# Attention in a fused layer: eight of eleven row-sum steps per head group leave TensorE for accumulating transfers into a side buffer

## The reference

```
scores = jnp.einsum('bshd,bthd->bhst', q / jnp.sqrt(jnp.float32(HEAD_DIM)), k)
scores = jnp.where(causal, NEG_INF, scores)
attn = jax.nn.softmax(scores, axis=-1)
ctx = jnp.einsum('bhst,bthd->bshd', attn, v)
```

## Time and profile before

| | |
|---|---|
| median of 3 runs | 2349.49 us (2347.68 to 2350.36) |
| the profiled execution | 2347.9 us, span 2346.0 us |
| busy TensorE / VectorE / ScalarE / GpSimd | 98% / 75% / 55% / 10% of the span |
| attention stage | about 340 to 1525 us |

### The profile page before, as it was taken

The page is one execution under the profiler, slowest core; times in us unless marked ns, Lnnn a source line. Parts: engine busy times, 40 slices in busy tenths (PEclk is TensorE's granted clock), DMA queues, the critical chain, the costliest instruction groups (busy, mean ns, idle before and its releaser), DMA issues.

```text
span 2346.0 us, 34451 instructions
## 1 busy us (share of the span) xinstructions
PE 2305.6 (98%) x12598; PEld 1417.8 (60%) x12598; DVE 1769.3 (75%) x1808; ACT 1295.7 (55%) x1638; POOL 240.5 (10%) x275
## 2 busy tenths in 40 slices
PE   9999989999999999999999999999999999999997
PEld 7888844444444444444444444478888888888886
DVE  7777759899898998989989999945556556465553
ACT  4444458888888888888888888811111111111111
POOL 2111111101111010211102111000000000000001
PEclk9999979999999999999999999999999999999999
DMA  7767794101811008210082101441102011110100
GB/s 248 262 243 254 240 270 97 38 6 28 172 42 41 16 15 168 55 33 24 6 165 67 33 24 40 145 156 37 42 31 66 19 60 36 37 54 19 37 19 20
DMA packets 126303, 197.49 MB, mean 84 GB/s; under 512 B 14489, under 2 KB 39577, under 8 KB 126113
## 3 DMA queue, kind: packets, MB, share of 16 engines
q1 hardware_dynamic: 126128, 195.25, 29.5%
HBM read 122.83 MB, written 72.37 MB: 83 GB/s over the span
## 4 chain that ended last, share of the span: by engine, by line
PE 92%; DMA 2%; ACT 2%; SPq 2%; DVE 2%; issue 1%; POOL 0%; ACTq 0%; DVEq 0%; POOLq 0%
PE score L977 24%; PE ctx_acc L993 21%; PE slot L1384 20%; PE y L1395 10%; PE acc L416 10%; PE slot L1325 3%; PE sums_acc L1001 2%; ACT probs L1052 1%; PE sums_acc L790 1%; PE turn L438 1%; DMA queries<-shift 1%; PE slot L1366 1%; SPq L76 0%; DMA wq_float<-wq_f 0%; DMA v_rows<-v_out 0%
## 5 line engine op out<-in xcount | busy, mean ns | idle before, releaser
L1052 ACT ACTIVATE probs<-score 128x1024 f32<-128x1024 f32 (+3 forms) x1152 | 1000.2, 968 | 174.7 <-PE score L977 171.7
L1113 DVE TENSOR_TENSOR total<-total,probs 128x2048 f32<-128x2048 f32 (+3 forms) x468 | 985.8, 2106 | 76.4 <-POOL probs L941 21.1
L977 PE MATMUL score<-queries,keys 98*128 98x512 f32 (+3 forms) x2304 | 641.8, 406 | 8.6 <-ACT probs L1052 4.3
L977 PEld LDWEIGHTS score<-queries,keys 98*128 98x128 f32 x2304 | 381.0, 189 | 430.5 <-ACT probs L1052 352.0
L1460 ACT ACTIVATE hidden<-slot,gate_scale_sb 128x512 f32<-128x512 f32 x128 | 88.3, 690 | 634.3 <-PE slot L1384 634.3
L993 PE MATMUL ctx_acc<-probs,values 128*32 128x512 f32 (+3 forms) x3584 | 422.3, 561 | 0.0
L1522 DVE SCALAR_TENSOR_TENSOR hidden<-slot,up_scale_sb,hidden 128x512 f32<-128x512 f32 x128 | 96.1, 751 | 255.6 <-ACT hidden L1460 255.6
L941 POOL TENSOR_SCALAR_AFFINE_SELECT probs<-probs 128x512 f32<-128x512 f32 x128 | 158.5, 1240 | 1010.3 <-ACT probs L1052 1010.3
L1384 PE MATMUL slot<-xt_hi,w_front 128*128 128x512 f32 x608 | 238.4, 392 | 1.5 <-DVE xt_lo L1563 1.5
L1384 PE MATMUL slot<-xt_lo,w_front 128*128 128x512 f32 x608 | 238.0, 391 | 0.0
L993 PEld LDWEIGHTS ctx_acc<-probs,values 128*32 128x32 f32 x3584 | 85.4, 108 | 194.1 <-issue 148.0
(11 more groups left out here) (142 smaller groups left out, 2193.8 us busy)
## 6 DMA issues: line engine op xcount, KB each, us to landing
keys<-k_hi SPq DMA_DIRECT2D x64, 256.0 KB
queries<-q_hi SPq DMA_DIRECT2D x64, 256.0 KB
wq_int<-in_wq SPq DMA_DIRECT2D x48, 256.0 KB, 3.3
wq_float<-wq_f SPq DMA_DIRECT2D x48, 256.0 KB, 2.8
x_raw<-in_x_t SPq DMA_DIRECT2D x32, 256.0 KB, 4.2
v_rows<-v_out SPq DMA_DIRECT2D x32, 256.0 KB, 2.1
k_hi<-part_hi SPq DMA_DIRECT2D x32, 256.0 KB, 2.0
k_lo<-part_lo SPq DMA_DIRECT2D x32, 256.0 KB, 2.4
```

Source lines behind the costliest of these rows:

```text
L977: ins = pe.matmul(score[u % RING][:, i, cut(t):], keys[0:ROWS, kb // ST, h, kb % ST * P:(kb % ST + 1) * P], queries[0:ROWS, q_buffer[ch], ...
L1052: act.activation(probs[:, t % PB, 2 * p:2 * p + 2, cut(t):], score[u % RING][:, :, cut(t):], ACT.Exp).then_inc(exped, 1)
L1113: dve.tensor_tensor(into, into, now, ALU.add).then_inc(added, 1)
```

## The change

TensorE keeps three summing steps in each group (`PE_SUMS = 3`), one in chunk 3 and two in chunk 4. In chunks 5 to 7 it has none. There every fourth late step, from the second late step on and none of the last six, is `queued`: places 9, 13, 17 of chunk 5, 9 to 21 of chunk 6, 9 to 25 of chunk 7, so 3 + 4 + 5 = 12 in a group. GpSimd issues a transfer of the step's 128x2048 exponentials, 1 MB, into a new buffer `side`: a plain copy for the first of a chunk, an accumulating transfer for the others, which adds to what is there. Each waits for the one before (`side_added`). ScalarE waits for the transfer before it writes the step's buffer again. Behind the third step from the chunk's end (`fold_at`, place 29 in chunk 7) VectorE adds `side` to `total` once (`folded`), and its next addition waits for that. The memory that is reserved for the descriptors of GpSimd's transfers is set to 4096 bytes, a size that the kernel before does not give.

```diff
-    PE_SUMS = 11
+    PE_SUMS = 3
+    QUEUED_FROM, EVERY, REST = 5, 4, 7
...
-    pe_sums = {late[(i + 1) * len(late) // PE_SUMS - 1] for i in range(PE_SUMS)}
+    early_late = [t for t in late if steps[t][0] < QUEUED_FROM]
+    pe_sums = {early_late[(i + 1) * len(early_late) // PE_SUMS - 1] for i in range(PE_SUMS)}
+    queued = [t for ch in range(QUEUED_FROM, NCH) for t in [x for x in late if steps[x][0] == ch][1:1 - REST:EVERY]]
+    fold_at = {last[ch] - 2: ch for ch in range(QUEUED_FROM, NCH)}
+    NQ, NF = len(queued), len(fold_at)
...
-    adds = [t for t in range(NS) if not by_pe(t)]
+    adds = [t for t in range(NS) if not by_pe(t) and t not in queued]
...
+        side = sb("side", [P, HG, CH])
...
+            def add_aside(g, t):
+
+                ch = steps[t][0]
+                opens = not any(steps[x][0] == ch for x in queued if x < t)
+                if opens:
+                    pool.wait_ge(folded, NF * g + folds_before(ch))
+                else:
+                    pool.wait_ge(side_added, 16 * (NQ * g + queued_before(t)))
+                pool.wait_ge(exped, 2 * NS * g + 2 * t + 2 + RING)
+                pool.nop(nofuse=True)
+                if opens:
+                    pool.dma_start(side[:], probs[:, t % PB, :, :]).then_inc(side_added, 16)
+                else:
+                    pool.dma_start(side[:], probs[:, t % PB, :, :], accum_op=ALU.add).then_inc(side_added, 16)
...
                     act.wait_ge(added, NA * g + adds_before(t - PB + 1) + A_CREDIT)
+                    if t - PB in queued:
+                        act.wait_ge(side_added, 16 * (NQ * g + queued_before(t - PB + 1)))
...
+                            if t - 1 in fold_at:
+                                dve.wait_ge(folded, NF * g + folds_before(ch) + 1)
...
+                    if t in fold_at:
+                        dve.wait_ge(side_added, 16 * (NQ * g + queued_before(last[ch])))
+                        dve.wait_ge(added, NA * g + adds_before(t + 1) + A_CREDIT)
+                        dve.tensor_tensor(total[:, ch % 2, :, :], total[:, ch % 2, :, :], side[:], ALU.add).then_inc(folded, 1)
...
-    nc = bacc.Bacc("TRN2", target_bir_lowering=False, num_devices=1)
+    nc = bacc.Bacc("TRN2", target_bir_lowering=False, num_devices=1, dynamic_dma_scratch_size=4096)
```

More of the change, by code:

```diff
@@ L702, in attend, with queued_before, folds_before @@
     late = [t for t in range(NS) if not diagonal(t) and place(t) >= 2 * ST]
-    pe_sums = {late[(i + 1) * len(late) // PE_SUMS - 1] for i in range(PE_SUMS)}
+    early_late = [t for t in late if steps[t][0] < QUEUED_FROM]
[3 more added lines that the diff above has]
+    NQ, NF = len(queued), len(fold_at)
+    assert not any(t in queued or t in pe_sums for t in fold_at)
+    def queued_before(t):
+        return sum(x < t for x in queued)
+    def folds_before(ch):
+        return max(0, ch - QUEUED_FROM)
     def by_pe(t):
         return t in pe_sums
-    adds = [t for t in range(NS) if not by_pe(t)]
+    adds = [t for t in range(NS) if not by_pe(t) and t not in queued]
     NA = len(adds)
@@ L751, in attend @@
         begun = sem("begun")
+        side_added = sem("side_added")
+        folded = sem("folded")
         totaled = sem("totaled")
@@ L933, in pool_attention, with mask @@
                             .then_inc(g_masked, 1)
+            def mask(g, t):
+                pool.wait_ge(exped, 2 * NS * g + 2 * t + 2 + RING)
+                view = probs[:, t % PB, :, cut(t):cut(t) + P]
+                pool.nop(nofuse=True)
+                pool.affine_select(out=view, in_=view, compare_op=ALU.is_ge, fill=0.0, base=0,
+                                   pattern=[[0, HG], [1, P]], channel_multiplier=-1).then_inc(masked, 1)
+            def add_aside(g, t):
[5 more added lines that the diff above has]
+                    pool.wait_ge(side_added, 16 * (NQ * g + queued_before(t)))
+                pool.wait_ge(exped, 2 * NS * g + 2 * t + 2 + RING)
+                pool.nop(nofuse=True)
+                if opens:
+                    pool.dma_start(side[:], probs[:, t % PB, :, :]).then_inc(side_added, 16)
+                else:
+                    pool.dma_start(side[:], probs[:, t % PB, :, :], accum_op=ALU.add).then_inc(side_added, 16)
             for g in range(NG):
@@ L936, in pool_attention @@
                     if diagonal(t):
[L938 to L942, removed]
+                        mask(g, t)
+                    elif t in queued:
+                        add_aside(g, t)
         def pe_attention(pe, general):
@@ L1104, in dve_attention @@
                     ch, kb = steps[t]
-                    if not by_pe(t) and (place(t) or not ch):
+                    if t in adds and (place(t) or not ch):
                         dve.wait_ge(exped, 2 * NS * g + 2 * t + 2 + RING)
```

## The result

| | before | changed |
|---|---|---|
| median | 2349.34 us (4 runs) | 2403.19 us (4 runs, 2402.58 to 2406.29) |
| ratio | | 1.0233, 95% interval 1.0221 to 1.0245 |
| profiled execution, span | 2347.9, 2346.0 us | 2403.6, 2401.8 us |

The change makes the kernel 54 us slower. Forecast were 25 us less, and the range ended at 2400.

A forecast was written before the change was run, and what follows sets the result against it. TensorE was taken to set the pace, VectorE a close second. 2347.9 - 27.5 (removed sums) + 2 (VectorE) = 2322.4 us profiled, so 2324 us median; own range 2317 to 2334, whole range 2317 to 2400 us.

The forecast's parts named there:

- The removed sums: Chunks 5 to 7: 32 summing steps fewer at 0.86 us, 27.5 us saved (1.72, 1.72, 3.44 us per chunk).
- The small bound: Lower figure for the removed sums from the matmul rows: 0.52 us a step, 16.7 us for 32 steps.
- VectorE: Chunks 5, 6, 7: VectorE needs 47.9, 54.2, 64.0 us against TensorE's 48.6, 56.75, 64.4, so it fits.
- The charge of 2 us: 0.5 us added for each group for a chunk start where VectorE's work doesn't fit; bounds nothing to 12 us.
- the two rivals on them: GpSimd issues lengthen additions by 0.48 us each: 2335 us, chance 0.07; issues wait up to 2.29 us for additions: 2362 us, 0.05.
- D where nothing competes: Time from a queued step's exponentials' end to its transfer's landing, chunks 5 and 6: 7.7 us, within the 8.25 us spacing.
- the prediction's other estimate: Accumulating transfer by the skill's fixed time and rate, at half rate: 2.0 + 2 x 2.4 = 6.8 us.
- I charge nothing: Chunk 7: accumulating transfers get a good part of the engines on their own queue, loads become late instead; 0 us.
- The first rival: Chunk 7, groups 0 to 2: loads hold transfers up, D 13.4 us, 40 us lost, 2364 us; chance 0.22.

The follow-up runs named there:

- chunk 4: Version for chunks 5 and 6 (TensorE sums four steps in chunk 7, nothing queued there) with two queued steps in chunk 4 too: 2328.98 us, ratio 0.9917.
- the kernel for chunks 5 and 6: The changed kernel with queued steps in chunks 5 and 6 alone; in chunk 7 TensorE sums four steps as before: 2338.17 us, ratio 0.9950.

## Why the prediction was wrong

- **The removed sums: right.** 0.86 us each, from the two lengths of a cycle. Chunk 5 lost 1.51, chunk 6 1.68 us, as 1.72 said; chunk 7 is at 64.47 us when the loads are small, 64.4 predicted. The small bound was misread: the 352 records of the matmul row are eight for each of 44 steps, so it gives 1.04 us a step and 33 us for 32, not 0.52 and 16.7, and is no lower bound. By the same count the 48 matmuls that the prediction expected in the trace are 96 records.
- **VectorE: right that it fits,** with the reason too narrow. I compared its occupancy with each chunk's length; it carries additions over, as chunk 4 showed. The charge of 2 us wasn't needed for chunks 5 to 7, though chunks 3 and 4, where a TensorE sum moved, grew by 0.2 to 0.5 us each, 2.05 us in all: that the charge of 2 us comes out is luck.
- **The issues and VectorE: the two rivals on them have fallen.** In the changed kernel from 583 to 641 us, with four issues in it, VectorE's additions read

```profile
L1154 DVE TENSOR_TENSOR total<-total,probs x15: 2291/2293/2293, 581.3 to 634.4; 128x2048 f32<-128x2048 f32 x15
```

which is as long as before. An issue that waits for exponentials starts 0.53 to 0.56 us after their end, though VectorE is adding most of the time. The Trainium skill, SBUF — State Buffer (Who interferes with whom), says that an addition with two inputs in SBUF holds up only what GpSimd reads; the trace agrees for these issues.
- **D where nothing competes: right.** 7.7 us was the estimate. Transfers land in a median of 7.0 us, with a copy at 4.5 (the kernel for chunks 5 and 6), which makes D 7.5; the issues are up to 10.0 us apart where one waits for the transfer before (chunk 6 of group 1 of the change), still below 10.3. That adding takes longer than copying, but not twice as long, was the right guess; the prediction's other estimate, 2.0 + 2 x 2.4 = 6.8 us, is 0.2 us below the landing measured. The Trainium skill, DMA: Bandwidth & Descriptors (Anatomy of one DMA), gives a fixed part of about 2.0 us and the bytes at 436 GB/s for a transfer that GpSimd issues; the estimate by it is 4.4 us for a plain 1 MB, and the trace agrees for the copy.
- **The step that failed: "I charge nothing" for chunk 7.** I took it that a transfer on its own queue gets a good part of the engines at once and that the loads become late instead. The runs show D at 14.5 us in its place, 12 to 13 even for a copy, and the dose: 8.0, 9.2 and 13.7 us to landing with a quarter, half and all of the loads. The loads do become late as well (a block of values lands after a median of 12.3 us in place of 7.2), but not instead. The share of 1.09 at 585 to 611 us was the warning; a separate queue is no separate engine. The Trainium skill says so in DMA: Bandwidth & Descriptors (Issuing engines are not separate DMA queues): transfers run on the same 16 engines and interleave, whichever engine started them; the runs above agree. The prediction used only the rate formula of that page.
- **The first rival had the place and the price, but not all of it.** Its D of 13.4 us was 1 us low. It counted three late transfers for three groups and 40 us; ScalarE's waits are 47 us in these groups. It left out the last group, whose weights (13.1 us to landing in place of 5.8) are what loads there: 10.8 us of waits at a share of only 0.53 before. No version loads fewer weights, so for this group the cause is read from the trace. And it had no term for what the waits cost beyond their length, 18.7 us, which goes with the lower clock. 2324 + 47 + 10.8 + 18.7 = 2400.5 us. The rest is at the end of the stage: from the last output of attention to the first gate row of the next stage it takes 30.0 in place of 26.2 us, because the last fold had waited for its transfer and TensorE then waits for VectorE:

```profile
1576.44 1.93 PE L807 MATMUL sums_acc<-total,ones 128*32 128x512 f32 x8 [3.15 <-DVE total L1154]
```

Open is by what rule the engines are shared: the loads of keys and values add about 7 to 8 us to either kind of transfer, but beside the weights the copies come out at 9.4 to 10.2 us from issue to issue. That the clock makes the 18.7 us rests on the rows above, not on a run that changes the clock alone.

## What to carry to other kernels

Before work goes to a transfer, read the transfer engines' share in the very stretch, not over the span, and treat a share near 1 as a queue that the new transfer joins, whoever issues it. Compare its landing there with the time until its buffer is wanted, and count each wait for more than its length on a TensorE that ran without pause: chunk 7 lost 1.2 to 1.5 times the waits in the versions with 7 us of them or more. If it doesn't fit, move the loads or the transfers: here the same idea is 2.3% slower with its last five transfers of each group beside the loads, and 0.5 to 0.9% faster without them.

## What the runs showed of the hardware

- A copy of 1 MB from SBUF to SBUF issued by GpSimd mostly lands in 4.4 to 4.7 us, and an accumulating transfer of the same size in 6.9 to 7.0, where no load or store is under way; beside the loads of keys and values they take a median of 12.3 and 13.7 us.
- In the kernel before, the loads of keys, queries and values move 204 GB/s at a share of 1.09 (585 to 611 us), those of the weights 295 GB/s at 0.80 (1480 to 1490 us). The share isn't the rate. The pieces of key loads write 32 partitions each; whether that makes the difference no run shows.
- The issue of a copy occupies GpSimd for 0.53 to 0.58 us (the first of the kernel for 0.78), that of an accumulating transfer for about 0.86 us.
- SyncE's own issues can take long: in chunk 7 of group 0 of the changed kernel the issue of one key load takes 9.13 us and that of another 5.50 us, against 0.3 to 1 us before. It happens where loads and the new transfers overlap; what SyncE waits for the trace doesn't show.

```profile
599.08 9.13 SPq L76 DMA_DIRECT2D keys<-k_hi  x1
```
